# Gate weights carried through DRAM, rows normalised on ScalarE, and x added by a DMA, in a graph layer with a small mixture of experts

## The reference, cut to what matters

```
h   = layernorm(x)
x1  = x + h @ W1.T + b1 + mean_over_edges(h[nbr]) @ W2.T + b2
n   = layernorm(x1)
gates = softmax(n @ gW + gb)                # 4 experts
w   = softmax(top-2 of gates)               # 2 weights a row, 0 for the other experts
out = x1 + shared_mlp(n) + sum_e w[e] * expert_mlp_e(n)      # relu layers 256-128-64-256, shared 256-256-128-256
```

## Time and profile before

| what | us |
|---|---|
| median of 3 runs | 3193.63 (3193.41 to 3203.1) |
| the profiled execution | 3189.69 |
| its span, first to last instruction | 3188.1 |
| busy PE / DVE / ACT / POOL | 3080.3 / 2688.2 / 1989.3 / 1844.3 |

### The profile page before, as it was taken

How to read it: one execution, slowest core, us unless ns; L and a number is a source line. 1 busy time by engine, 2 the same in 40 slices (tenths; PEclk the granted TensorE clock), 3 DMA queues, 4 the chain that set the end, 5 groups by cost and what they waited for, 6 DMA issues and landing times.

```text
span 3188.1 us, 61476 instructions
## 1 busy us (share of the span) xinstructions
PE 3080.3 (97%) x20817; PEld 2819.6 (88%) x20817; DVE 2688.2 (84%) x7211; ACT 1989.3 (62%) x3507; POOL 1844.3 (58%) x1554
## 2 busy tenths in 40 slices
PE   7999899999699999999999999999999999999998
PEld 7999899999678888888888889898888888888887
DVE  8988888885288888888888888888888888888886
ACT  5656556556456666666666666666666666666665
POOL 1788888888665555555555555554545455555540
PEclk9999999999899999999999999999999999999999
DMA  7777767677533333333333333333333333333320
GB/s 242 214 225 207 202 194 208 200 192 212 150 98 99 87 95 91 93 92 94 92 95 90 95 90 95 90 92 93 90 94 88 98 87 99 86 100 87 98 79 27
DMA packets 201824, 387.38 MB, mean 122 GB/s; under 512 B 106671, under 2 KB 109821, under 8 KB 201506
## 3 DMA queue, kind: packets, MB, share of 16 engines
q1 hardware_dynamic: 133906, 226.02, 26.1%
q10 hardware_dynamic: 30800, 102.42, 10.0%
q0 software_dynamic: 36800, 54.95, 7.4%
HBM read 236.11 MB, written 161.00 MB: 125 GB/s over the span
## 4 chain that ended last, share of the span: by engine, by line
PE 71%; DVE 1%; ACT 0%; DMA 0%; issue 0%; POOL 0%; POOLq 0%; DVEq 0%
PE acc L1136 25%; PE acc L1197 13%; PE acc L1097 13%; PE acc L1117 4%; PE acc L1119 4%; PE acc L1183 3%; PE acc L1160 3%; PE acc L1193 2%; PE acc L1152 1%; PE acc L1108 1%; PE acc L1146 1%; DMA rows<-z_d,tab 0%; ACT h2f L1237 0%; DVE e_lo L1335 0%; DVE x1n_sb L1423 0%
## 5 line engine op out<-in xcount | busy, mean ns | idle before, releaser
L165 POOL DMA_INDIRECT rows<-z_d,tab x500 | 580.9, 1162 | 571.7 <-DMA tab<-tab_d 437.7
L1136 PE MATMUL acc<-x1T_hi,wl_hl 128*128 128x500 f32 x2400 | 657.2, 389 | 0.0
L177 POOL TENSOR_SCALAR e_oh<-iota_sb,tab 128x250 fp32r<-128x250 f32 (+1 forms) x500 | 523.8, 1058 | 228.7 <-PE acc L1119 218.2
L386 POOL DMA_INDIRECT tab_d<-pair,idx x400 | 549.1, 1373 | 118.6 <-issue 111.1
L725 PE MATMUL acc<-w_hl,xT_hi 128*125 128x256 f32 x3200 | 573.1, 284 | 0.0
L1224 ACT ACTIVATE h1f<-acc,bl_sb 128x500 f32<-128x500 f32 x600 | 407.7, 679 | 246.5 <-PE acc L1136 228.6
L1136 PEld LDWEIGHTS acc<-x1T_hi,wl_hl 128*128 128x128 f32 x2400 | 444.5, 188 | 84.0
L1197 PE MATMUL acc<-wl_hl,h_hi 128*125 128x256 f32 x2400 | 483.5, 282 | 0.0
L1396 DVE TENSOR_TENSOR h_lo<-h1f,h_hi 128x500 fp32r<-128x500 f32 x600 | 392.4, 673 | 104.3 <-ACT h_hi L1231 104.3
L725 PEld LDWEIGHTS acc<-w_hl,xT_hi 128*125 128x125 f32 x3200 | 468.9, 189 | 0.0
L1197 PEld LDWEIGHTS acc<-wl_hl,h_hi 128*125 128x125 f32 x2400 | 392.0, 186 | 3.7
(11 more groups left out here) (144 smaller groups left out, 6287.9 us busy)
## 6 DMA issues: line engine op xcount, KB each, us to landing
xs<-in_x SPq DMA_DIRECT2D x100, 448.0 KB
z_d<-zs ACTq DMA_DIRECT2D x100, 448.0 KB
y_d<-ys ACTq DMA_DIRECT2D x100, 448.0 KB
y_sb<-y_d SPq DMA_DIRECT2D x100, 448.0 KB
x_sb<-in_x SPq DMA_DIRECT2D x100, 448.0 KB
out<-x_sb SPq DMA_DIRECT2D x100, 448.0 KB
codes_b<-code_d SPq DMA_DIRECT2D x25, 390.6 KB
rows<-z_d,tab POOLq DMA_INDIRECT x500
```

Source lines behind the costliest of these rows:

```text
L165: pool.indirect_dma_start(out=rows[g.h][:, q, :], out_offset=None, in_=z_d, in_offset=bass.IndirectOffsetOnAxis(ap=tab[g.h][:, q, 0:1], ax ...
L177: pool.tensor_scalar(e_oh[:, q, w], iota_sb[:, w], tab[g.h][:, q, 1:2].bitcast(F32), None, ALU.is_equal).then_inc(S["e_oh_ready"], 1)
L386: pool.indirect_dma_start(out=tab_d, out_offset=bass.IndirectOffsetOnAxis(ap=idx[:, n:n + 1], axis=0), in_=pair[:, 2 * n:2 * n + ROW], in_ ...
L1136: mm = pe.matmul(bank[L1_BANKS[t]][:, 0:GN], wl1_hl[:, w, f, t * P:(t + 1) * P], (x1T_hi, x1T_lo)[a][:, f, :], start=n == 0, stop=n == 5)
```

## The change

Four edits in stage 2; stage 1 keeps its work (only the constants for the 0/1 matrix go).

1. **Gates.** DVE writes the four weights of a row, their high and their low part side by side into `wst` (128 x 64), and turns it in 32 x 32 blocks into `wst_T`. SP stores that with four DMAs into a small DRAM tensor `gate_d`, waits, and loads it back: four DMAs that each repeat one expert's 500 weights over 64 partitions (`gbc`), and two that bring the high and low rows as operand of the bias product (`wT_r`). The transposes and spreading matmuls of PE and the copy of ACT go; the gating product reads `gbc` in SBUF.
2. **Normalised rows.** `x1n_sb` is made by ACT as Identity(x1 * rstd + nb), nb = -mean * rstd from a new small DVE operation. It is made at the end of the step before the one that uses it, and stands in ACT's queue ahead of the next step's first relu.
3. **Table.** The load of the edge table stands ahead of the gates' DMAs and the output store.
4. **x.** No load of x by SP and no vector addition: POOL issues an accumulating DMA of 125 x 1024 from x onto `y_sb`, once y has landed, ahead of its gathers.

PE's and ACT's order changes too: the transposes of `x1n_sb` come right after layer 1, and all of layer 2 after them; ACT does `x1T_hi` ahead of layer 2's relu. DVE does the statistics in one go, and the output rows between the gate operations, so that the gate weights are the last thing in its step.

```diff
             def step_tensor(pe, i):
...
-                    pe.wait_ge(S["gates_ready"], i.n(1, 1))
-                    if i.c:
-                        pe.wait_ge(S["out_ready"], i.n(2))
-                    for s in range(NS):
-                        mm = pe.transpose(bank[6][0:NB3, s * SP_:(s + 1) * SP_], wst[:, s, :],
-                                          ident_sb[0:SP_, 0:SP_])
-                    mm.then_inc(S["wT_done"], 1)
-                    layer2(0)
-                    pe.wait_ge(S["wT_ready"], i.n(1, 1))
-                    for t in range(2):
-                        pe.matmul(bank[6 + t][:, 0:GN], selg_r[:, t, :], wT_r[:],
-                                  start=True, stop=True).then_inc(S["gate_bc_done"], 1)
-                    layer2(1)
                 if nxt:
                     pe.wait_ge(S["x1n_ready"], n1.n(NS, NS))
...
                 if back:
-                    layer2(2)
+                    for t in range(H2T):
+                        layer2(t)
...
                         if s == 0:
+                            pe.wait_ge(s_gw, i.n(32, 32))
+                            if i.c:
+                                pe.wait_ge(S["out_ready"], i.n(2))
                             pe.wait_ge(S["h2_lo_ready"], i.n(H2T, H2T))
...
             def step_scalar(act, i):
...
-                        if t == H1T - 1:
-                            act.wait_ge(S["wT_done"], i.n(1, 1))
-                            act.copy(wT_r[0:NB3], bank[6][0:NB3, 0:GN]).then_inc(S["wT_ready"], 1)
                         h1_high(t)
-                    h2_value(0)
-                    h2_high(0)
-                    h2_value(1)
                 if nxt:
...
                 if back:
+                    h2_value(0)
+                    h2_value(1)
+                    h2_high(0)
                     h2_high(1)
...
+                if front:
+                    act.wait_ge(S["l2_nb_ready"], g.n(1, 1))
+                    if g.c:
+                        act.wait_ge(S["x1T_done"], g.n(FT))
+                    for s in range(NS):
+                        act.activation(x1n_sb[:, s, :], x1_sb[g.u][:, s, :], ACT.Identity,
+                                       bias=l2_nb[:, s:s + 1], scale=l2_rstd[:, s:s + 1])\
+                           .then_inc(S["x1n_ready"], 1)
...
             def gates_weights(dve, i):
...
-                gate_step(dve, i, 11, dve.tensor_tensor(gd[:], gd[:], r4, ALU.mult))
-                gate_step(dve, i, 12, dve.tensor_copy(wst[:, :, 0:NX].bitcast(F32R), gd[:]))
-                dve.tensor_copy(wst[:, :, 2 * NX:3 * NX].bitcast(F32R), gd[:])\
-                   .then_inc(S["gates_own"], 1)
-                dve.tensor_tensor(wst[:, :, NX:2 * NX], gd[:], wst[:, :, 0:NX],
-                                  ALU.subtract).then_inc(S["gates_ready"], 1)
+                    dve.wait_ge(S["gates_turned"], i.n(1))
+                gate_step(dve, i, 11, dve.tensor_tensor(
+                    w_own.rearrange("p (e s) -> p s e", s=NS), gd[:], r4, ALU.mult))
+                gate_step(dve, i, 12, dve.tensor_copy(w_hi.bitcast(F32R), w_own))
+                gate_step(dve, i, 13, dve.tensor_tensor(w_lo.bitcast(F32R), w_own, w_hi,
+                                                        ALU.subtract))
+                if i.c:
+                    dve.wait_ge(s_gst, i.n(64))
+                dve.transpose(wst_T[:], wst[:]).then_inc(S["gates_turned"], 1)
...
             def step_vector(dve, i, more):
...
                 def gated(t):
-                    dve.wait_ge(S["gate_bc_done"], i.n(2, t + 1))
+                    dve.wait_ge(s_gbc, i.n(64, 64))
                     dve.wait_ge(S["h2_relu_ready"], i.n(H2T, t + 1))
-                    dve.tensor_tensor(h2f[t][:], h2f[t][:], bank[6 + t][:, 0:GN],
+                    dve.tensor_tensor(h2f[t][:], h2f[t][:], gbc[t][:],
                                       ALU.mult).then_inc(S["h2_gated"], 1)
...
                 if back:
+                    gated(0)
+                    gated(1)
+                    h2_low(0)
+                if front:
+                    if g.c:
+                        dve.wait_ge(S["x1n_ready"], g.n(NS))
+                    wait_alone(dve, s_xl[g.h], g.half(16))
+                if back:
                     h2_low(1)
                     h2_low(2)
                 if front:
                     graph_vector(dve, g, more)
+                    graph_stats(dve, g)
                 if nxt:
                     gates_logits(dve, n1)
+                if back:
+                    out_rows(0)
                 if nxt:
                     gates_softmax(dve, n1)
                 if front:
+                    dve.wait_ge(S["l2_rstd_ready"], g.n(1, 1))
+                    dve.scalar_tensor_tensor(out=l2_nb[:], in0=l2_mv[:, :, 0], scalar=-1.0,
+                                             in1=l2_rstd[:], op0=ALU.mult,
+                                             op1=ALU.mult).then_inc(S["l2_nb_ready"], 1)
+                if back:
+                    out_rows(1)
                 if nxt:
                     gates_rank(dve, n1)
                     gates_weights(dve, n1)
...
+            def spread_gates(sp, i):
+                wait_alone(sp, S["gates_turned"], i.n(1, 1))
...
+                for b in range(4):
+                    n = min(32, SP_ - 32 * b)
+                    sp.dma_start(gate_d.rearrange("c r p -> r c p")[:, :, 32 * b:32 * b + n],
+                                 wst_T[32 * b:32 * b + 32, :].rearrange("r (c p) -> r c p", c=2)
+                                 [:, :, 0:n]).then_inc(s_gst, 16)
+                wait_alone(sp, s_gst, i.n(64, 64))
...
+                for e in range(NX):
+                    sp.dma_start(gbc[e // 2][e % 2 * 64:e % 2 * 64 + 64, :],
+                                 gate_f[e * GN:(e + 1) * GN].partition_broadcast(64))\
+                      .then_inc(s_gbc, 16)
...
             def step_sync(sp, i, more):
...
                     load_y(sp, i + 4)
+                if (i + 5).exists():
+                    load_table(sp, i + 5)
+                if (i + 1).exists():
+                    spread_gates(sp, i + 1)
...
-                if (i + 5).exists():
-                    load_table(sp, i + 5)
+
+            def add_x(pool, g):
+                wait_alone(pool, s_yl[g.h], g.half(LOAD))
+                pool.dma_start(y_sb[g.h][:], g.of(x_v), accum_op=ALU.add).then_inc(s_xl[g.h], 16)
 
             def step_pool(pool, i):
+                if (i + 3).exists():
+                    add_x(pool, i + 3)
                 if (i + 4).exists() and i.c != -2:
                     gather(pool, i + 4)
```

More of the change, by code:

```diff
@@ L63, in build @@
 def build(nc, x, src, dst, w1t, w2t, b12, wl1, bl1, wl2, bl2, wl3, b3, gw, gb,
-          ident, iota, codes, selg, tie, out, y_d, z_d, code_d, tab_d, tabx_d,
-          agg_x, cnt_x):
+          ident, iota, codes, low, tie, out, y_d, z_d, code_d, tab_d, tabx_d,
+          agg_x, cnt_x, gate_d):
     with ExitStack() as ctx:
@@ L346, in _ @@
                                 sp.dma_start(st_b3[:], b3).then_inc(s_wl, 16)
-                                sp.dma_start(st_sel[:], selg).then_inc(s_wl, 16)
+                                sp.dma_start(st_low[:], low).then_inc(s_wl, 16)
                                 sp.dma_start(iota_sb[:], iota).then_inc(s_cst, 16)
@@ L1045, in build @@
             y_sb = [sb(f"y_sb{h}", [SP_, NS, D], F32, c2) for h in range(2)]
-            x_sb = [sb(f"x_sb{h}", [SP_, NS, D], F32, c2) for h in range(2)]
             x1_sb = [sb(f"x1_sb{h}", [SP_, NS, D], F32, c2) for h in range(U)]
@@ L1064, in build @@
             l2_rstd = sb("l2_rstd", [SP_, NS], F32, c2)
+            l2_nb = sb("l2_nb", [SP_, NS], F32, c2)
             deg = sb("deg", [SP_, NS], F32, c2)
@@ L1074, in build @@
             gpair = sb("gpair", [SP_, NS, NX, NX], F32, c2)
-            wst = sb("wst", [SP_, NS, NB3], F32, c2)
+            wst = sb("wst", [P, 2 * 32], F32, c2)
+            wst_T = sb("wst_T", [P, 2 * 32], F32, c2)
+            gbc = [sb(f"gbc{t}", [P, GN], F32, c2) for t in range(2)]
+            w_own = wst[0:SP_, 0:16]
+            w_hi = wst[0:SP_, 16:32]
+            w_lo = wst[0:SP_, 32:48]
             more_sb = sb("more_sb", [SP_, NS, D], F32, c2)
@@ L1370, in graph_vector, with graph_stats @@
                         op0=ALU.mult, op1=ALU.add).then_inc(S["x1_ready"], 1)
-            def graph_stats(dve, g, part):
-                for k in part:
-                    s = S_ORDER[k]
+            def graph_stats(dve, g):
+                for k, s in enumerate(S_ORDER):
                     wait_alone(dve, S["x1_ready"], g.n(NS, k + 1))
@@ L1409, in h2_low, with out_rows @@
                                       ALU.subtract).then_inc(S["h2_lo_ready"], 1)
-                if back:
-                    h1_low(0)
+                def out_rows(j):
+                    dve.wait_ge(S["l3_done"], i.n(2, j + 1))
+                    dve.tensor_tensor(
```

(26 more changed lines are left out.)

79 lines of the change are left out of this document (35 added, 44 removed).

## The result

| | before | after |
|---|---|---|
| time, median of 20 runs each, same chip | 3198.56 us (3193.41 to 3204.07) | 3206.93 us (3200.35 to 3216.86) |
| profiled execution, span | 3188.1 us | 3203.1 us |
| mean spacing of 94 steady steps | 22.90 us | 22.91 us (21.99 to 26.11) |
| chain that ended last: share of PE | 71% | 21% |

A forecast was written before the change was run, and what follows sets the result against it. PE bounds stage 2 at 22.90 us a step; with 22.10 taken, 99 spacings save 79 us, start and end add 8.5, giving 3123 us. Likeliest case 3105 to 3167, overall range on to 3200.

The forecast's parts named there:

- PE's list: PE's own instructions in a stage 2 step: 0.89 us leaves, so a PE-bound step goes from 22.90 to 22.01 us.
- The loop through POOL and ACT: Stage 2 chain from edge sums through one-hots, rstd, activations and layer 2 back to edge sums: 21.95 us.
- Start and end: Fill and end of stage 2: later first x1n and a stall in the first full step, +8.5 us, from 3 to 13.
- rival (1): Loop through POOL and ACT is 0.4 to 0.9 us longer, step 22.5 to 23.0; chance 0.15, half of it faster.
- (4): Rival that the edits don't take hold; excluded for PE, whose instructions are gone from its queue; no chance given.
- the gates' way through DRAM: Turned weights stored to DRAM and loaded back for the gating product: 7.8 us, hidden, ends 6.5 and 10.75.
- Leg one: The gates' four small stores to DRAM on SP: last issue at 1.3, then 2.4 us, loads going out at 3.7.
- rival (2): Gates come too late: DMAs over 9.2 us lengthen the step, 23.65 us and 3276 at the upper bound; chance 0.15.
- rival (3): Accumulation holds a few DMA engines long, slowing the gates' loads by 1.9 us: step 22.6, 3172 us; chance 0.08.
- Leg two: Four repeating loads of the gates from DRAM, 500 KB: 0.8 + 2.2, 0.6 landing, 0.5 for gathers, 4.1 us.
- The limit: How long the gates' DMAs may take in a step: 8.4 us unseen, up to about 9.2 before PE waits.
- The hidden case: The forecast itself, gates' DMAs hidden in the step: 22.1 us a step, own range 3105 to 3167 us; chance 0.62.

The follow-up runs named there:

- E3: Changed kernel with the repeating loads reading a constant DRAM table, issued ahead of the gates' stores without waiting for them (work left out): 3120.74 us.
- E2: Changed kernel with POOL's accumulating DMA of x issued behind its five gathers instead of ahead of them: 3127.16 us, ratio 0.9795.
- E4: Changed kernel with x loaded by SP and added by DVE again, just ahead of the gating product, no accumulating DMA: 3169.79 us.
- E9: Changed kernel with the repeating gate loads bringing 250 of 500 columns from the second group on (work left out): 3126.87 us.
- E8: Changed kernel with POOL's DMA of x as a plain load into its own buffer, x left out of the sum: 3141.60 us.

## Why the prediction was wrong

**What held.** PE's list lost 0.89 us: the shortest steps are 21.98 to 22.00, forecast 22.01. The loop through POOL and ACT did not lengthen the step: with the gates out of the way, 22.03 (E3). The activations took 2.06 for four, the one-hots 5.3 on the mean (forecast 5.22), the weights were turned at 3.52 (forecast 3.6), the transposes stood at 8.16 (8.16). Start and end together cost 9.0 us (2.55 + 8.43 - 2.02) against 8.5, but that the sums agree is partly luck: the first full step cost 8.4, where 4.5 had been given, the time to the first layer-1 matmul 2.6, where 4 had, and the end gave back 2.0, which the forecast had not. (PE's first transposes stood at 891.72, not 886, but 6.2 of this lie ahead of stage 2; within it they came 3.5 later, forecast 4.) The first full step stalls behind POOL's gathers, since rstd is now needed in the same step. So rival (1) fell, and so did (4).

**The step that failed** is the gates' way through DRAM, "In all 7.8 us: hidden". It is 9.97 and not hidden: in 70 of 100 steps the gating product waits more than 0.2 us for gbc, and over all steps DVE stands idle ahead of it for 1.33 us on the mean. Two terms of it were too small:

- Leg one, "I take 2.4, since nothing stands ahead in SP's queue": 3.7 in all, measured 4.12. Nothing stood in SP's queue, but on POOL's the accumulating DMA had been issued some 2.4 us earlier. The prediction priced it at "Nothing for it, from 0 to a lengthening of the gates' loads by 2 us". The sum asked only when its data were wanted; what they stand beside was left to that bound and to rivals (2) and (3), and the bound names the gates' loads, where it was the stores that were hit (leg two is the same with and without the accumulation, 5.82 and 5.94). By themselves the four stores and their landing take 2.92 (E2, E4), less than forecast; the accumulation adds 1.20. The changed kernel's steps, sorted by how long ahead of the gates' stores the accumulation was issued, agree with this: the third with the shortest lead (1.93 on the mean) has a leg one of 4.64, the middle one (2.47) 4.01, the last (2.82) 3.69. And the lead is short where POOL had waited longest for y; it waited 38 times in 1000 us.
- Leg two, "4.1", measured 5.82. The loads' issues are 0.60 us apart, not 0.43 (four in 2.37), which makes up to 0.5. E9 puts the bytes at 1.7, under the 2.2 assumed, so the remaining 1.7 (5.82 - 4.1) is that 0.5, 0.5 less for the bytes, and some 1.7 in start-up, landing and gathers above what I gave them. How these divide no experiment tried, but the packets of the changed kernel's trace say something: the first one of the gbc loads starts 1.3 us after the first issue, where the forecast gave 0.8; the data ends at 4.7 to 5.2, where 0.8 + 2.2 + 0.5 gave 3.5; and the product follows at 5.8, so landing is about the 0.6 assumed or up to 1.1. The start and the stretch of the data beside the gathers were too short, more than the landing.

By the figures of the Trainium skill (DMA: Bandwidth & Descriptors, Anatomy of one DMA), which that section states for a DMA issued by GpSimd while these are issued by SP, leg one was estimated at 3.3 us, and undisturbed it is 2.92: for a small transfer that was nearer than my middle of 3.7. For leg two the estimate was 3.2, and the trace has 5.8: the figure prices one DMA, and here four are issued, beside five gathers.

**The limit was about right.** The prediction put PE's first wait at a way of 9.2 us, gated at 12.8, with each microsecond above it lengthening the step. E4, where the lateness is nearly the same in every step, fits: gated at 13.36 it should take 22.1 + 0.56 = 22.66, and takes 22.63. Across the kernels, gated at 11.76, 12.28, 12.72 and 13.49 gives 22.03, 22.14, 22.30 and 22.91: scatter of single steps costs a little from 12.2 on, and between the last two points 0.77 us of lateness make 0.61 of the step. What happened is rival (2) in kind, and rival (3) in part: the accumulation is in it, but not as engines few and long held. From 2059 to 2060, where the trace has packets of no other queue, the DMA share is 0.99 of all 16 engines, which five engines could not make. So the engine count of 5 for 125 rows that rival (3) took from the Trainium skill (DMA: Bandwidth & Descriptors, Why a DMA increments its semaphore by 16 and not by 1) is not seen on this DMA; the exception for some copies of GpSimd that the same section makes would fit. At 9.97 the way ended just under the 10.0 from which rival (2) "costs more than before": the 0.89 us that PE gave up was spent to the last tenth on waiting.

**Why the range missed.** The two ends of the way were on paper, 6.5 and 10.75, and the limit of 9.2 between them. My middle of 7.8 took 2.4 where the only small transfer in the rows had 3.65, behind a store of 500 KB: I set the company aside as the row's own and gave the gates almost none. The hidden case got 0.62 and the late one 0.15. With two serial transfers, one of them beside a DMA that the change itself adds, the two should have stood about level.

## What to carry to other kernels

A transfer that is needed only 35 us later is free only for whoever waits for it; ask also which short transfer on a chain it will share the engines with. Where a chain goes to DRAM and back within a step, count all issues of it at their own length, give each leg the company it will have, and keep other queues' bulk DMAs out of that stretch: here the accumulation issued 10.9 us later in the step turned +0.3% into -2.1%. When an operand is wanted in the same step instead of the next, look through the fill as well: what stands ahead of its producer there was free before and is not now.

## What the runs showed of the hardware that was not expected

- An accumulating DMA (500 KB of float32 from DRAM onto SBUF) occupies the engines for 51.9 engine-us, 3.2 us of all 16, a plain load of the same rows for 32.5, 2.0 us (differences of the queue's time between kernels; E8 and the kernel before).
- Behind it, the wait for four stores of 8 KB on another queue ended 1.2 us later on the mean, 0.5 us later behind the plain load. Their issues on SP got longer too (3.07 us for four in the step shown, 1.84 in E2's); why was not tried.
- SP's issue of a repeating load of 64 x 500 takes 0.60 us (the middle one of 400; four in 2.37), that of a small store 0.43.
- The accumulation's row on POOL is 1.0 us of issue, as for an indirect gather.
